# Expert weights split ahead of the waiting steps, and the first steps of the attention re-ordered, in a two-layer network kernel

## The reference

```python
x = x + mamba2(gate(x, f, cond))        # layer 0, "attn"
x = x + moe(gate(x, f, cond))           # layer 0, "ffn": 8 experts, top 2
x = x + attention(gate(x, f, cond))     # layer 1: 16 query heads in 4 groups, width 128, causal
x = x + swiglu(gate(x, f, cond))        # layer 1, "ffn": inner width 1408

def gate(r, k, v):                      # k = v = f
    ek = exp(min(k, 30)); ekv = ek * v; euk = exp(min(u + k, 30))
    nf, df = forward scans of ekv, ek   # a = a * decay + ekv_t, along the 512 tokens
    nb, db = backward scans of ekv, ek
    return sigmoid(r) * (nf + nb - ekv + euk * v) / max(df + db - ek + euk, 1e-8) * (0.8 + 0.2 * tf)

def expert(x):                          # for each token its two best experts, weighted
    h = x @ w1.T + b1
    y = h[0::2] * sigmoid(1.702 * h[0::2]) * (h[1::2] + 1)
    return y @ w2.T + b2
```

## Time and profile before

| | |
|---|---|
| median of 3 runs | 2612.58 us (2611.5 to 2615.99) |
| profiled execution | 2612.03 us, span 2610.2 us from first to last instruction |
| TensorE busy | 2298.4 us (88%) |
| VectorE, ScalarE, GpSimd busy | 1884.8 (72%), 944.9 (36%), 686.2 us (26%) |
| chain of waits by engine | PE 43%, issue 28%, POOL 9%, DVE 8% |
| mean granted TensorE clock | 0.954 of full speed |

### The profile page before, as it was taken

One profiled execution on the slowest core, in us unless ns is written; L12 is line 12 of the kernel. 1 busy time (PEld: TensorE's weight loads), 2 busy tenths in 40 slices (PEclk: granted clock), 3 DMA queues, 4 the chain that ended last, 5 costly groups with the idle time before them and its releaser, 6 DMA issues.

```text
span 2610.2 us, 33671 instructions
## 1 busy us (share of the span) xinstructions
PE 2298.4 (88%) x10507; PEld 1712.0 (66%) x10524; DVE 1884.8 (72%) x2875; ACT 944.9 (36%) x1956; POOL 686.2 (26%) x545
## 2 busy tenths in 40 slices
PE   0789979989897899799767899999999998999998
PEld 0344444454455778677557787887888876788886
DVE  8988898989886765666544557777787776566665
ACT  2243342342532332342333344444444444322222
POOL 5434434344341543344321002212212210000000
PEclk9899999999998999899878999999999999999999
DMA  5000001010023432333232000000001111000001
GB/s 203 17 33 33 33 16 49 16 45 19 32 81 131 154 113 80 112 129 112 101 125 61 1 28 20 16 26 17 31 0 41 48 32 49 25 24 24 24 12 65
DMA packets 50491, 142.10 MB, mean 54 GB/s; under 512 B 4768, under 2 KB 4768, under 8 KB 46064
## 3 DMA queue, kind: packets, MB, share of 16 engines
q1 hardware_dynamic: 31872, 89.89, 9.8%
q10 hardware_dynamic: 12864, 32.81, 3.4%
q0 software_dynamic: 5680, 18.62, 2.4%
HBM read 106.95 MB, written 34.34 MB: 54 GB/s over the span
## 4 chain that ended last, share of the span: by engine, by line
PE 43%; issue 28%; POOL 9%; DVE 8%; POOLq 5%; ACT 3%; DMA 1%; ACTq 1%; another core or an unknown queue 0%; SPq 0%; DVEq 0%
PE bank L341 9%; PE bank L343 9%; PE bank L342 9%; PE bank L2278 4%; PE bank L2277 4%; PE bank L2279 4%; PE bank L2231 3%; POOLq L494 2%; POOL g_v L495 2%; POOL g_v L502 2%; PE bank L2272 1%; POOLq L520 1%; POOLq L506 1%; POOLq L517 1%; POOL g_eu L501 1%
## 5 line engine op out<-in xcount | busy, mean ns | idle before, releaser
L2106 PE MATMUL bank<-um,w_in 128*128 128x512 f32 x576 | 265.4, 615 | 6.4 <-DVE lm L1479 6.2
L2106 PEld LDWEIGHTS bank<-um,w_in 128*128 128x128 f32 x576 | 110.6, 197 | 138.8 <-issue 127.3
L341 PE MATMUL bank<-u_hi,aw_hi 128*128 (+1 forms) x384 | 158.7, 413 | 15.4 <-DVE k_lo L1857 11.7
L1112 ACT ACTIVATE probs<-bank,nmx 128x128 f32<-128x128 f32 (+3 forms) x256 | 131.5, 527 | 90.7 <-DVE nmx L1876 90.7
L1119 ACT ACTIVATE pt_hi<-bank 128x512 fp32r<-128x512 f32 (+1 forms) x192 | 94.0, 526 | 161.3 <-PE bank L2231 161.3
L343 PE MATMUL bank<-u_hi,aw_lo 128*128 (+1 forms) x384 | 152.3, 397 | 0.0
L342 PE MATMUL bank<-u_lo,aw_hi 128*128 (+1 forms) x384 | 152.2, 396 | 0.0
L2231 PE MATMUL bank<-ident,probs 128*128 128x128 f32 x640 | 96.5, 283 | 56.5 <-DVE pt_lo L1891 28.8
L341 PE MATMUL bank<-u_hi,fw_hi 128*128 128x512 f32 x352 | 136.9, 389 | 0.0
L342 PE MATMUL bank<-u_lo,fw_hi 128*128 128x512 f32 x352 | 136.9, 389 | 0.0
L343 PE MATMUL bank<-u_hi,fw_lo 128*128 128x512 f32 x352 | 136.9, 389 | 0.0
(11 more groups left out here) (388 smaller groups left out, 6232.6 us busy)
## 6 DMA issues: line engine op xcount, KB each, us to landing
m_stage<-in_moe SPq DMA_DIRECT2D x21, 1024.0 KB, 5.2
y_slot<-m_o ACTq DMA_DIRECT2D x39, 256.0 KB, 2.6
g_v<-in_fT SPq DMA_DIRECT2D x18, 512.0 KB, 3.4
gates<-g_v SPq DMA_DIRECT2D x18, 512.0 KB, 2.8
f_stage<-in_ffn SPq DMA_DIRECT2D x11, 768.0 KB, 4.4
u_g<-gates SPq DMA_DIRECT2D x8, 1024.0 KB, 5.6
aw_in<-in_att SPq DMA_DIRECT2D x4, 1280.0 KB, 6.2
w_in<-in_w_in ACTq DMA_DIRECT2D x1, 4640.0 KB, 16.8
```

Source lines behind the costliest of these rows:

```text
L341: nc.tensor.matmul(out, hi_w, hi_x, start=start, stop=False)
L1112: A(probs[:, h % 2, PR_AT[qb]:PR_AT[qb] + w], S_[bk][:, c0:c0 + w], ACT.Exp, bias=nmx[:, h % 2, qb:qb + 1], scale=SCALE, accum_out=rsum[:, ...
L2106: mm = M(dst[:], w_in[:, k, c0:c0 + P], um[:, k, :], start=(k == 0), stop=(k == KC - 1))
```

## The change

Four things are re-ordered. (1) In the expert stage ACT and DVE treat the first weight piece ahead of by_hi and by_lo and the second ahead of the tanh work; the flag and the number of the expert are read from the table in the block before, not at the head of each half trip and in the branch. (2) The scans of a gate pair are written as forward in one block and backward at the head of the next, and `dens` stands ahead of the reciprocal. (3) SP issues the first weight part ahead of the gate values of sequence 0, and the store of the gate pair right behind these; TensorE gets 44 products without use (`keep_busy`) ahead of the first combine. (4) The input of sequences 1 to 3 is prepared in pieces: the tanh stays where it was, the rest is placed between the steps of the second head of the pass.

The diff, cut to its core:

```diff
@@ SP, attention's start
-            for b in range(BATCH):
+            att_load(0, 0)
+            fetch_gate(2, 0, u_g[:, :, 0:T], g_fetched[0])
+            g_store(sp, G_ATT - 1, LATE)
+            sp.wait_ge(cb_T, TB)
+            att_load(0, 2)
+            att_load(0, 1)
+            for b in range(1, BATCH):
                 fetch_gate(2, b, u_g[:, :, b * T:(b + 1) * T], g_fetched[b])
-                if b == 0:
-                    att_load(0, 0)
-                    sp.wait_ge(cb_T, TB)
-                    att_load(0, 2)
-                    att_load(0, 1)
-            g_store(sp, G_ATT - 1, LATE)
@@ ACT, block_act
+            def next_expert(j, last):
...
+                return (act.value_load(entry(2, j), min_val=0, max_val=1),
+                        act.value_load(entry(1, j + 1), min_val=1, max_val=E - 1))
...
-                act.wait_ge(ty_done, j + 1)
-                A(by_hi[:].rearrange("p k t -> p (k t)"), TP[:], ACT.Copy).then_inc(by_hi_ready, 1)
-                if not (last and q == 2):
-                    with act.If(flags[q] != 0):
-                        e = act.value_load(...)
+                if last and q == 2:
+                    inner_hi()
+                else:
+                    flag, e = nxt
+                    with act.If(flag != 0):
                         act.wait_ge(dn_done, FIRST + j)
                         split_hi(e, e % 2, (0,))
+                        inner_hi()
+                        split_hi(e, e % 2, (1,))
                         up_tanh(j + 1, (q + 1) % 3)
-                        split_hi(e, e % 2, (1,))
+                        split_hi(e, e % 2, (2,))
                         if not (last and q >= 1):
                             u_hi_copy(j + 2)
-                        split_hi(e, e % 2, (2,))
                     with act.Else():
+                        inner_hi()
                         up_tanh(j + 1, (q + 1) % 3)
...
+                more = (q < 1) if last else (h, q) != (1, 2)
+                nxt = next_expert(j + 1, last) if more else None
                 act.wait_ge(dn_done, FIRST + j + 1)
@@ ACT, loop
+                nxt = next_expert(pair * 6, False)
                 for h in range(2):
-                    flags = [act.value_load(...) for q in range(3)]
@@ ACT, att_act
                 probs_exp(i, 1)
+                if mod in (1, 2):
+                    input_hi(mod + 1)
...
                 if first:
                     gated_input(1)
-                    spread_weights(2)
...
                 probs_exp(i, 2)
+                if first:
+                    input_hi(1)
+                    spread_weights(2)
                 q_hi_copy(i, 3)
@@ DVE, block_dve
-                if (h, q) == (0, 2):
-                    dens((k, s))
+                if (h, q) == (0, 1):
+                    backward((k, s), 0)
+                elif (h, q) == (0, 2):
+                    backward((k, s), 1)
...
                         split_lo(e, e % 2, (0,))
+                        inner_lo()
+                        split_lo(e, e % 2, (1,))
                         glu(j + 1, (q + 1) % 3)
-                        split_lo(e, e % 2, (1,))
                         next_inner(j, q, last)
                         split_lo(e, e % 2, (2,))
...
                 if (h, q) == (0, 0):
-                    scans((k, s), 0)
+                    forward((k, s), 0)
                 elif (h, q) == (0, 1):
-                    scans((k, s), 1)
+                    forward((k, s), 1)
                 elif (h, q) == (0, 2):
+                    dens((k, s))
                     inverse((k, s))
@@ DVE, att_dve
                 pt_lo_split(i, 0, (2,))
+                if mod in (1, 2):
+                    gated_input(mod + 1)
...
                 normalise(i, 1)
+                if mod in (1, 2):
+                    input_lo(mod + 1)
...
                 pt_lo_split(i, 1, (2,))
+                if first:
+                    gated_input(1)
...
                 q_lo_split(i, 3)
                 normalise(i, 2)
+                if first:
+                    input_lo(1)
                 ctx_lo(i, 1)
@@ PE
+            keep_busy(44)
             batch_T(0)
```

More of the change, by code:

```diff
@@ L1786, in next_inner, with next_expert, entry, forward @@
                     u_lo_split(j + 2)
-            def block_dve(pair, h, q, flags, last):
+            def next_expert(j, last):
+                def entry(row, at):
+                    return tab[0:1, row, at:at + 1] if last else tab[0:1, row, bass.ds(at, 1)]
+                return (dve.value_load(entry(2, j), min_val=0, max_val=1),
+                        dve.value_load(entry(1, j + 1), min_val=1, max_val=E - 1))
+            def forward(pair, t):
+                for i in range(2):
+                    gate_forward(dve, *pair, t, i)
+                gate_edge(dve, *pair, t)
+            def backward(pair, t):
+                for i in range(2):
+                    gate_backward(dve, *pair, t, i)
+            def block_dve(pair, h, q, nxt, last):
                 j = pair * 6 + (3 * h + q)
-                dve.wait_ge(by_hi_ready, j + 1)
-                V.tensor_tensor(flat(by_lo[:]), TP[:], flat(by_hi[:]).bitcast(F32), ALU.subtract).then_inc(y_split, 1)
                 k, s = moe_pair(pair)
-                if (h, q) == (0, 2):
-                    dens((k, s))
-                if not (last and q == 2):
-                    with dve.If(flags[q] != 0):
-                        e = dve.value_load(tab[0:1, 1, j + 1:j + 2] if last else tab[0:1, 1, bass.ds(j + 1, 1)], min_val=1, max_val=E - 1)
+                def inner_lo():
+                    dve.wait_ge(by_hi_ready, j + 1)
+                    V.tensor_tensor(flat(by_lo[:]), TP[:], flat(by_hi[:]).bitcast(F32), ALU.subtract).then_inc(y_split, 1)
+                if (h, q) == (0, 1):
+                    backward((k, s), 0)
+                elif (h, q) == (0, 2):
+                    backward((k, s), 1)
+                if last and q == 2:
+                    inner_lo()
+                else:
+                    flag, e = nxt
+                    with dve.If(flag != 0):
                         split_lo(e, e % 2, (0,))
+                        inner_lo()
+                        split_lo(e, e % 2, (1,))
                         glu(j + 1, (q + 1) % 3)
-                        split_lo(e, e % 2, (1,))
                         next_inner(j, q, last)
@@ L1814, in block_dve @@
                     clamp((k + 1, s), 1)
+                more = (q < 1) if last else (h, q) != (1, 2)
+                return next_expert(j + 1, last) if more else None
             split_lo(0, 0, (0,))
```

38 lines of the change are left out of this document (24 added, 14 removed).

## The result

The changed kernel takes 2574.32 us (median of 4 runs, 2570.7 to 2577.34). The kernel before took 2613.98 us on the same chip. The ratio is 0.9852, with a 95% interval of 0.984 to 0.9865: 39.7 us less, where 35 us were forecast (2577 us). The profiled execution is the slowest of the four, 2577.34 us with a span of 2575.3, so the two traces differ by 34.9 us (2610.2 to 2575.3).

What follows compares the result with a forecast made beforehand. TensorE, busy 88% of the span, was taken as the bound, so gains come from its idle stretches. The parts, 15 + 0 + 16 + 4 = 35 us, take 2612.0 to 2577 us; range 2565 to 2594 us.

Steps and rivals of the forecast that it cites:

- Part 1: Expert stage: splitting weight pieces ahead of waiting steps saves 15 us, 8.5 of it in block 22; bounds 7 to 20.
- part 2: Expert stage: writing the scans two by two leaves the executed order unchanged and costs 0.
- The small terms: Expert stage: gains of the splitting blocks other than 22: 2.6, 0.8, 0.8, 0.9, 1.2 and 0.2 us.
- rival B: Expert stage: by_lo comes late, first blocks stall inside, only block 22 gains; 2585 us, or 2591 with slow clock; 15%.
- costed at nothing: Expert stage: two table reads per block are free, under ACT's 2.4 us idle time and DVE's sequencer reading ahead.
- The bound I gave for the other case: Expert stage, reads not covered: by_lo starts at 4.9 instead of 3.4 us after the transposes; TensorE needs it from 5.7.
- Rival D: Expert stage: table reads hold their engines in every block, 50 us lost against 35 gained; 2627 us; 5%.
- Part 3: Attention's start: earlier gate store and weight part, plus fill, save 13.8 + 2.4 = 16.2 us; bounds 11 to 18.
- rival A: Attention's start: fill products run at half clock to 1309.9, so combines start 5.4 us later; 2583 us; 10%.
- E: Attention's start: ACT still waits for the store, as gathers share the engines; costs at worst 5 us; 2582 us; 5%.
- Part 4: Sequences 1 to 3: split inputs gain 9.5 us in 2 and 3, lose 5.5 in 1; bounds 0 to +9.
- rival C: Sequence 1's input split hides better than counted, or the clock follows removed waits everywhere; 2568 us; 10%.

Runs made afterwards that it cites:

- e_scans_together: Changed kernel with the dispatched gate's forward, edge and backward scans in a row again in their two blocks; 2564.12 us, ratio 0.9838.
- e_products_first: Changed kernel with GpSimd's two pairs of gate products ahead of the first two gathers of each six blocks; 2576.02 us, ratio 0.9854.
- e_one_piece: Changed kernel with sequence 1's input prepared in one piece as before, sequences 2 and 3 still split; 2572.83 us, ratio 0.9843.
- e_experts: Kernel before with the expert stage's edits alone (weight split, early table reads, scans two by two); 2593.3 us, ratio 0.9948.
- e_start: Kernel before with the attention's start alone (gate store and weight part ahead of later inputs, 44 fill products); 2590.36 us, ratio 0.9937.
- e_both: Changed kernel with the dispatched gate's scans back in their two blocks and sequence 1's input in one piece; 2561.51 us, ratio 0.9815.
- e_fill88: Changed kernel with 88 products of fill instead of 44 ahead of the first combine; 2569.7 us in one run, no ratio.

## Why the prediction was right, point by point

**Part 1 (15 us forecast), with part 2 (0): 11.8 us.** Block 22 gave 8.4 us for 8.5. The first up product starts 1.2 us earlier behind the block's start, not 1.7, and the wait at the second is gone. That the two numbers meet is partly luck, for like code shows block 22 at 17.3 to 18.9 us, a gain of 8.4 to 10.0. The small terms were too low in sum: without blocks 1 and 22 the stage gave 9.5 us, where I had 6.5. Blocks 28, 35 and 24 gained (1.5, 2.3 and 1.7 us), since the stall went from their starts. Each splitting block together with the one behind it gave 0.6 us (4), -0.4 (18), 1.6 (23), 3.3 (27) and 2.6 (34), for 0.8, 0.9, 0.2, 2.6 and 0.8. Against that stands block 1, 6.1 us worse, on which I had nothing. The wait on by_lo, of which rival B spoke, is real: 12.5 us against 4.6 before, 5.4 of it in block 1. Part of the stall did move inside the blocks, so that bu_lo's wait fell to 4.8 us, under the 8 to 10 named as a sign, and the two waits together only from 19.9 to 17.3. But other blocks than 22 gained too, where rival B gave them nothing.

**The reads "costed at nothing".** The step that failed is that VectorE's sequencer "reads ahead while a scan runs": by the change's order the reads stand behind the edge step, and each pair leaves VectorE idle for 1.5 us. Where the reads stand behind two scans, they do cost nothing (e_scans_together). The bound I gave for the other case held (by_lo at 4.9 us): in the plain blocks (0, 1) and (0, 2) by_lo starts 4.95 and 5.04 us behind the transposes, and they last 9.8 us as forecast. It cost some 1.5 to 3.5 us in the blocks on the edge. Part 2's "cost 0" fell with it: the execution order is the same, but what lies in the pause isn't. Rival D, 50 us for the same cause, is out.

**Part 3 (16 us): 16.5 us** in the profile, 16.0 alone. Both terms of its sum held. The second query product starts 14.0 us earlier behind block 38's start (54.4 to 40.4 us; in the traces it starts at 1337.00 and 1310.13), for 13.8 forecast, and its twelve products take 2.9 us instead of 5.4, which is 2.5 for 2.4. By the runs, the place of the store is 13.8 of the 16.5 within one series (68.5 against 54.7 in e_products_first and e_one_piece), 14.5 against the changed kernel, the quicker products behind the stall included. The 2 to 3 us ahead of it aren't assigned: the fill alone is at most 1, no run tests the earlier weight part alone, and e_experts, which has none of these edits, has 68.4 us in this stretch instead of 70.5. Rivals A and E are out: the fill ran at 0.22 us a product, and the store landed in 3.1. The half pace that rival A's sum rests on isn't twice the first pace as the text says: 0.43 us is twice 0.22, while twice the 0.23 of the earlier trace rows is 0.46, or 20.2 us for 44.

**Part 4 (4 us): 9.3 us.** Sequence 1 loses 5.0 us for the 5.5 forecast, and its new wait is 8.8 us, near the 7 forecast and under the 10 that I had named as the mark of an error. The mis-sized term is sequences 2 and 3: 9.5 forecast, 14.5 measured (6.7 and 7.8). I had counted the waits (10.0 us) and not the clock behind them, which was the second half of rival C. The last of the three stretches, before and after:

```profile
1487.12:1523.07 35.95, 29.28 (x174) 25.79 (x173) 17.32 (x27) 10.00 (x18) 0.00 (x0) 0.91 0.00 0
```
```profile
1456.28:1484.44 28.16, 26.99 (x174) 24.09 (x173) 16.95 (x27) 9.90 (x18) 0.00 (x0) 1.00 0.00 0
```

The same 174 products take 2.3 us less, at a granted clock of 1.00 instead of 0.91. The wait of 5.6 us and the slow products make up the 7.8.

**The sum.** 35 forecast. The medians give 39.7, the profiles 34.9. The errors are -3 in the expert stage, +0.5, +5, -3.7 in the rest and +1 ahead of block 0. That they cancel to nothing in the profiles is luck.

What the rest lost is explained only in part. It has two levels: about 1087.5 us in six kernels, and 1089 to 1091 in the other eight. The three kernels without the edits of the expert stage are all on the lower level. The other eleven lose 0.9 to 1.4 us at each of two heads, the 30th and the 46th, and some take it back later. The rows there show ScalarE: ahead of its copy into vT it stands idle for 4.0 to 4.5 us in all eleven, and nothing in the profile releases it, where it waits 2.2 us for a product in the other three. The changed kernel, and e_start:

```profile
1720.84 0.60 ACT L1118 ACTIVATE vT<-bank 128x512 f32<-128x512 f32 x1 [4.26 <-issue]
```
```profile
1733.29 0.60 ACT L1095 ACTIVATE vT<-bank 128x512 f32<-128x512 f32 x1 [2.19 <-PE bank L343]
```

In the 9 us around it more instructions are loaded, by the list of transfers of 1716 to 1725 us in the changed kernel and 1731.5 to 1740.5 in e_start:

```profile
q14 instruction: 5, 0.04, 1.1%
```
```profile
q14 instruction: 2, 0.02, 0.4%
```

So ScalarE may be waiting for its own instructions, which the edits have shifted. That isn't shown: no experiment was made on it, and the two heads cover 2.6 of the 3.7 us.

## What to carry to other kernels

When a stall goes, count the slow products behind it too: two waits of 10.0 us together were worth 14.5. A step split to let others pass is only worth it where its result isn't wanted at once; the same edit gave 14.5 us in sequences 2 and 3 and cost 5 in sequence 1. Put a table read behind a long operation of the same engine, where it costs nothing, and not behind a short one. Move a store that others wait for ahead of loads that nobody needs yet.

## What the runs showed of the hardware that was not expected

**A wait that goes with the series.** The combine of sequence 1 ends with four additions on VectorE, 1.8 us apart. In the changed kernel's profile the last comes late:

```profile
1342.07 0.69 DVE L1897 TENSOR_TENSOR XT<-XT,bank 128x512 f32<-128x512 f32 x1 [1.10 <-issue]
1347.38 0.69 DVE L1897 TENSOR_TENSOR XT<-XT,bank 128x512 f32<-128x512 f32 x1 [4.63 <-remote]
```

In e_scans_together, with the same instructions there, it does not:

```profile
1337.56 0.69 DVE L1895 TENSOR_TENSOR XT<-XT,bank 128x512 f32<-128x512 f32 x1 [1.10 <-PE bank L2408]
1339.35 0.69 DVE L1895 TENSOR_TENSOR XT<-XT,bank 128x512 f32<-128x512 f32 x1 [1.10 <-PE bank L2408]
```

In series 1 and 3 this wait was 4.5 to 4.6 us in all six profiles, in sequences 1 and 2. In the four of series 2 it was absent, and in series 4 it was 3.1 us (in e_both only in sequence 2). It follows the series and not the kernel, and its cause is open. TensorE's last product of that combine had ended at 1343.8, and GpSimd's next gather, which waits for the same signal, is as late (1347.62), so the signal is late and not VectorE. It moves 6 to 8 us between profiles of like code, as 162.5 and 164.1 against 170.0 us in the table. Only ratios within a series can be trusted at this size.

**GpSimd beside VectorE.** Before the change a product of GpSimd (L493) took 1.29 us in one place of block 0 and 3.35 in another, both beside VectorE's weight split, whose subtractions took 3.44 and 2.62 us there instead of 2.29. In the changed kernel GpSimd paused for 4.95 us between two products in block 0, with only its sequencer in a drain (L494), while VectorE had no break over 0.1 us. Spans on GpSimd are rough, so part of that pause may be the product itself. Block 1 took 18.0 to 18.1 us in five kernels with the same code up to there and 14.7 in the sixth, e_fill88, where GpSimd's products fell earlier. That their place beside the split decides was not tested by itself.
